# A decoder kernel with one engine's program written out in the Mamba stage, and one transposition moved in the feed-forward stage

## The reference, cut to what matters

```python
# Mamba layer, cut: 512 inner channels, 16 states
dt = softplus(log_dt @ W_dt.T + b_dt)
A_bar, Bu = exp(dt[..., None] * A), dt[..., None] * B_coef[:, :, None, :] * xc[..., None]
h = A_bar_t * h + Bu_t                      # for each position t
y_t = sum over states of h * C_t
y = (y + xc * D) * silu(z)
# quantised feed-forward, cut: 256 -> 1024 -> 256
def bitlinear(x, w): return act_quant(x) @ weight_quant(w).T
out = bitlinear(silu(bitlinear(x, w_gate)) * bitlinear(x, w_up), w_down)
```

## Time and profile before

| what | value |
|---|---|
| median of 3 runs | 3803.97 us (3803.84 to 3806.27) |
| the profiled execution, its own time | 3800.63 us |
| span of its trace, first to last instruction | 3797.8 us |
| mean granted TensorE clock | 0.95 of full speed |
| PE, DVE, ACT, POOL busy, share of the span | 87%, 82%, 74%, 68% |

### The profile page before, as it was taken

The page is one execution under the profiler, slowest core; times in us unless marked ns, Lnnn a source line. Parts: engine busy times, 40 slices in busy tenths (PEclk is TensorE's granted clock), DMA queues, the critical chain, the costliest instruction groups (busy, mean ns, idle before and its releaser), DMA issues. The chain is left out here.

```text
span 3797.8 us, 75246 instructions
## 1 busy us (share of the span) xinstructions
PE 3290.3 (87%) x23328; PEld 2494.5 (66%) x23360; DVE 3118.3 (82%) x5163; ACT 2817.2 (74%) x5141; POOL 2567.5 (68%) x2971
## 2 busy tenths in 40 slices
PE   8996988979963688999988989898899879997887
PEld 5664666668542477777767777777777757775565
DVE  5665999955386699999899989989999849998887
ACT  2222777854475799899898998989899737776887
POOL 1222767730086599888888988898898936665676
PEclk9998999979976899999999999999999989998999
DMA  2112222242213111121111211111111112322111
GB/s 61 55 55 56 44 53 49 50 106 46 52 34 85 37 52 57 50 54 53 54 53 56 57 50 57 49 53 56 55 52 51 48 47 68 77 54 64 51 61 45
DMA packets 285549, 209.62 MB, mean 55 GB/s; under 512 B 131416, under 2 KB 249752, under 8 KB 285224
## 3 DMA queue, kind: packets, MB, share of 16 engines
q1 hardware_dynamic: 285224, 205.72, 19.9%
HBM read 149.18 MB, written 51.41 MB: 53 GB/s over the span
## 5 line engine op out<-in xcount | busy, mean ns | idle before, releaser
L2896 POOL TENSOR_TENSOR ma_ch<-ma_h,ma_crep 128x512 f32<-128x512 f32 x1024 | 1348.2, 1340 | 190.5 <-DVE ma_h L3007 159.8
L3007 DVE TENSOR_TENSOR_SCAN ma_h<-ma_a,ma_pbu 128x512 f32<-128x512 f32 x1024 | 1196.5, 1203 | 123.5 <-PE ma_pbu L2576 108.1
L2576 PE MATMUL ma_pbu<-ma_ident,ma_bu 128*128 128x128 f32 x4096 | 655.6, 284 | 120.6 <-DVE ma_h L3007 92.6
L2576 PEld LDWEIGHTS ma_pbu<-ma_ident,ma_bu 128*128 128x128 f32 x4096 | 481.5, 144 | 349.2 <-DVE ma_h L3007 204.3
L2785 ACT ACTIVATE ma_a<-ma_dt,ma_A 128x510 f32<-128x510 f32 x1024 | 672.8, 711 | 1.3 <-issue 1.3
L2585 PE MATMUL ma_py<-ma_ident,ma_ch 128*128 128x128 f32 x4096 | 623.9, 278 | 9.8 <-DVE ma_gT L3025 7.8
L2778 ACT ACTIVATE ma_bu<-ma_uT,ma_b_t 128x512 f32<-128x512 f32 x864 | 555.6, 711 | 13.0 <-PE ma_pbu L2576 11.3
L2585 PEld LDWEIGHTS ma_py<-ma_ident,ma_ch 128*128 128x128 f32 x4096 | 493.4, 145 | 14.3 <-DVE ma_gT L3025 11.4
L1576 POOL TENSOR_TENSOR xa_prob<-xa_e,xa_rec_head 128x616 f32<-128x616 f32 x128 | 155.6, 1217 | 126.4 <-DVE xa_rec_head L1668 114.2
L924 POOL TENSOR_TENSOR xa_prob<-xa_e,xa_rec_head 128x616 f32<-128x616 f32 x128 | 155.7, 1217 | 107.0 <-DVE xa_rec_head L1016 90.4
L362 POOL TENSOR_TENSOR la_veps<-la_mv,la_eps 128x2 f32<-128x2 f32 x32 | 6.3, 196 | 248.8 <-DVE la_mv L395 248.8
(11 more groups left out here) (375 smaller groups left out, 7942.3 us busy)
## 6 DMA issues: line engine op xcount, KB each, us to landing
ma_crep<-ma_ct_dram SPq DMA_DIRECT2D x256, 256.0 KB
xa_x<-act SPq DMA_DIRECT2D x64, 256.0 KB, 2.7
act<-xa_y SPq DMA_DIRECT2D x64, 256.0 KB, 2.2
la_x<-in_x SPq DMA_DIRECT2D x32, 256.0 KB, 2.8
act<-la_y SPq DMA_DIRECT2D x32, 256.0 KB
act<-ea_x SPq DMA_DIRECT2D x32, 256.0 KB, 4.0
ma_x<-act SPq DMA_DIRECT2D x16, 512.0 KB, 4.5
ma_xr<-act SPq DMA_DIRECT2D x16, 512.0 KB
```

What stands on the lines that cost most here:

```text
L2576: last = pe.transpose(pbu[c % 2][:, t * P:(t + 1) * P], bu[:, s % 2, t, c * P:(c + 1) * P], ident[:, :])
L2896: pool.tensor_tensor(ch[:, s % 2, c], h[:, s % 2, c], crep[:, s % 4, :], ALU.mult).then_inc(multiplied, 1)
L3007: dve.tensor_tensor_scan(out=h[:, s % 2, c, :], data0=a[:, s % 2, c, :], data1=pbu[c % 2][:, :], initial=0.0, op0=ALU.mult, op1=ALU.add).t ...
```

## The change

Two edits, both in PE's programs. In the Mamba stage PE's 16 groups are written out one behind the other, with constant parity and constant wait values; the other engines keep their loops. In the feed-forward `turn_x` of an even slot moves from behind the up projection to behind the gate projection.

```diff
@@ mamba, TensorE
-            groups(pe, group)
+            for g in range(NG):
+                group(g, g % 2, g == 0, g == NG - 1)
             for late in range(K - LAG, K):
@@ bit_ffn, TensorE, slot
                     pe.wait_ge(g_ready, count(n2))
                     project(n2, 0, pgate, gate_made)
+                if not odd and n4 is not None:
+                    turn_x(n4)
                 if n is not None:
                     turn_h(n)
                 if n_1 is not None:
@@
                     pe.wait_ge(h_ready, count(n2))
                     project(n2, 1, pup, up_made)
-                if not odd and n4 is not None:
-                    turn_x(n4)
```

## The result

The changed kernel takes 3776.13 us, the median of 4 runs (3772.69 to 3779.92), against 3803.9 us (3802.32 to 3806.27, 4 runs) for the kernel before: a ratio of 0.9927, interval 0.991 to 0.9944. The forecast was 3786 us in a range of 3774 to 3797. In two later comparisons the changed kernel took 3776.78 and 3776.36 us, so its time is firm; the kernel before took 3798.2 and 3799.9 there (3797.4 and 3800.4 in two more), so the gain is 27.8 us in the first comparison and 21.4 and 23.5 us in the other two. The kernel before was at its slowest in the first.

What follows compares the result with a forecast made beforehand. Bounds: feed-forward, a PE-ACT wait cycle with DVE next; Mamba boundaries, PE's and DVE's jumps. Gains 13.5 + 4.4 = 17.9 us: span 3797.8 - 17.9 = 3779.9, + 2.8 = 3782.7, + 3.3 to the median: 3786 us, range 3774 to 3797.

Steps and rivals of the forecast that it cites:

- two bounds: Feed-forward: the PE-ACT wait cycle at 8.09 us a pair and DVE's work at 8.12, expected to coincide; 8.17 taken.
- DVE's own 8.12: Feed-forward: DVE idles 0.50 us of each 8.62 us pair, so a pair cannot go below 8.12 us.
- the ring: Feed-forward: the cycle of waits through PE and ACT from even ph to even ph, forecast at 4.12 + 3.97 = 8.09 us.
- 0.05 us a pair: Feed-forward: allowance for two closing bounds disturbing one another, in the 8.17 us taken for a pair.
- B: Feed-forward: another wait, say DVE's hscale, closes the cycle; gain only 0.1 us a pair, time 3797 us; chance 0.10.
- C: Feed-forward: px ahead of even ph costs 0.34 us a pair, not returned; time 3810 or 3814 us; chance 0.05.
- the sixth jump's price: Mamba: at the sixth jump only PE still jumps, so writing it out returns the whole 2.4 us.
- So I take 0.4 us at each of the five: Mamba: where DVE's jump stays, removing PE's returns 0.4 us each, between 0 and 1.2; 2.0 us in all.
- up to 8 us: Mamba: the gain if PE keeps its full clock after standing for DVE.
- The mid-group row: Mamba: profile row where PE, after standing 2.83 us far from any jump, ran at 1.2 GHz for 3.3 us.
- Rival A: Mamba: PE's jumps were the whole stall, so all 14.6 us return; time 3776 us; chance 0.20.
- Rival D: Mamba: the written-out program starves PE of instructions, 0.5 us in each of 16 groups; time 3794 us; chance 0.02.

Runs made afterwards that it cites:

- px_twice: The changed kernel with the four px transpositions done twice at their new place; 3785.43 us (one run).
- dve_no_jump: The changed kernel with DVE written out in both the Mamba stage and the feed-forward; 3768.64 us, ratio 0.992.
- mamba_only: The kernel before with only PE's 16 Mamba groups written out, feed-forward unchanged; 3792.46 us, ratio 0.9984.
- dve_alone: The kernel before with DVE's Mamba groups written out instead of PE's, feed-forward unchanged; 3804.94 us, ratio 1.0018.

## Why the prediction was right, and where it was off

**Feed-forward, 13.5 us forecast, 14.1 measured.** Right in size, and by its own steps. ACT's wait for `px` is gone, `xT` follows `scaled`, and PE's way from odd to even `ph` took on the `px`. The pair was forecast at 8.17 us from two bounds, a ring of 8.09 and DVE's own 8.12. Measured are 8.00 for the ring (`px_twice`: 8.44 less the 0.44 added) and 8.14 for DVE in the loop. `dve_no_jump` shows DVE's share of the bound: written out, DVE needs no more than 8.00 either. So the two bounds do stand on top of each other there, as forecast, each about 0.1 us lower. What was not foreseen is that part of DVE's 8.12 is not its work but its loop. That the two bounds disturb one another, for which 0.05 us a pair had been added, did not show: from the third to the 61st `h` a pair took 8.13 us on average, 8.60 before. PE's stand of 0.40 us ahead of the odd `ph` belongs to the ring as forecast (4.12 us for 3.53 of work, measured 4.09). Rivals B and C are refuted: ACT did wait for `hscale`, but 6.8 us in all, where B and C needed the whole gain to go there.

**Mamba, 4.4 us forecast, 7.1 measured in the profiled pair, 5.8 in the medians of `mamba_only`.** The mechanism was right: DVE's jump stays and is as long as before, the sixth jump's price came back but for 0.5 us (112.87 to 110.92 us, 2.0, forecast 2.4), and PE stands for DVE. The mis-sized step is this term: "So I take 0.4 us at each of the five". It took the half clock behind DVE's stand as certain, from a row of a stand in mid-group. The runs showed it in 11 of 30. Worked out: in the loop a jump cost 2.59 us on average (12 of them), 15.5 us for six. Written out, 5 x (0.37 x 2.5 + 0.63 x 1.1) + 0.3 = 8.4 us. The gain is then 7.1 us, and the six written-out traces have it: 1741.4 on average against 1748.7 for the two with the loop, 7.3 us. By these prices most of the gain at the five jumps is not time in which DVE waited for PE's branch, but a slow stretch of PE that often did not come. Had the half clock been certain, it would have been 15.5 - 5 x 2.5 - 0.3 = 2.7 us. The prediction had named this way out, "up to 8 us", and given it no chance of its own. One reading in it is off without effect: PE's median branch of 3574 ns counts the seventh, which falls through; the six that jump have 3768.

The mid-group row was a poor model for the jumps. In the six written-out traces PE stands 2.7 us in mid-group 78 times, and 72 of these stands have the half clock within the 5 us behind them. Here is one of them in the changed kernel, and the stand behind the fifth jump, with a window of 5 us behind each:

```profile
2460.35 0.63 PE L2576 MATMUL ma_pbu<-ma_ident,ma_bu 128*128 128x128 f32 x4 [2.68 <-DVE ma_h L3008]
...
2499.37 0.66 PE L2576 MATMUL ma_pbu<-ma_ident,ma_bu 128*128 128x128 f32 x4 [2.70 <-DVE ma_h L3008]
```

```profile
2460.30:2465.30 5.00, 4.81 (x28) 4.44 (x29) 5.00 (x9) 5.00 (x8) 4.85 (x5) 0.66 0.09 33
...
2499.40:2504.40 5.00, 5.00 (x44) 4.76 (x45) 4.72 (x5) 3.15 (x6) 4.85 (x4) 1.00 0.14 54
```

The stands are equally long and the outcome differs.

**Rival A is refuted, although its number, 3776, is the measured time.** It said that PE's jumps were the whole stall and 14.6 us would return. `mamba_only` gave 5.8 us, DVE still stands at five jumps, and `dve_alone` shows the reverse case: PE's jump alone costs all that the two cost together. **Rival D** is refuted too: a stretch without a jump takes 110.16 us with PE written out and took 110.32 before.

**From 3782.7 to the median.** The two stages gave 21.2 us for 17.9 forecast. The span was forecast at 3779.9 and came at 3778.1; the profiled execution was forecast at 3782.7 and took 3779.92 (1.8 us outside the span in place of 2.8). The other 7.1 us of the miss are in the step from there to the median: before, the profiled execution stood 3.3 us below it, after, 3.8 us above. The draw of the clock at five jumps, 1.4 us each, explains a spread of that size, up to 7 us between none and all; that it is what happened in these very runs is not shown, since only one of them has a trace.

**Luck in the range.** The range for the forecast by itself was 3781 to 3796 us, and the median of 3776.13 lies below it. It lies within 3774 to 3797 only because the range was stretched to take in rival A's lower end, and rival A is refuted. By stages the steps held, each gain inside its own bounds; that the total did too is partly luck.

**Not settled.** Why DVE's written-out groups take 0.4 us longer in the Mamba stage, while its written-out waits save 0.14 us a pair in the feed-forward. And what decides whether the clock is halved after a stand. Neither the length of the stand nor the kernel alone does; where it stands matters (72 of 78 in mid-group, 11 of 30 behind DVE's jump, 16 of 18 behind PE's own jump, with `dve_alone`), and no run shows why. That the 1.4 us between the two prices are caused by the clock is read from the windows and prices together; no run sets the clock.

## What to carry to other kernels

Where several engines jump back at the same point of a loop, their jumps run beside each other, and writing one engine out returns little more than the difference between the longest and the next (here the rest was a slow stretch of PE that often did not come); read each engine's branch and the first instruction behind it before pricing. Of the ways to be rid of the rest, more groups a turn kept the fast body and the short jumps elsewhere; writing every engine out in the Mamba stage alone gave the gain back and more (3779.97 us against 3776.78); writing DVE out in both stages was the fastest (3768.64). When an in-order engine waits for a transfer between two others, moving its producer is worth the ring's saving less what the producer costs in its new place, down to the next engine's own time; doubling the moved work shows at once whether it is on the ring.

## What the hardware showed that was not expected

- The same small loop's jump on DVE took 0.3 us or 3.3 to 3.6 us, with nothing changed but what was written ahead of it.
- A taken jump over the Mamba body, from branch to the first instruction of the new turn, took 3.4 to 4.2 us on DVE, 3.4 to 4.4 on PE, 2.5 to 3.5 on POOL, 2.4 to 2.9 on ACT, and 0.2 to 0.3 on SP.
- After a stand of 2.5 to 3.3 us behind DVE's jump PE had half the clock in 11 of 30 cases, in traces of one kernel 3 of 5 and 1 of 5; after one of 2.7 us in mid-group, in 72 of 78. The Trainium skill, "TensorE: Matmul & The Clock Gate", part 1, says that how many matmuls run slow at a kernel's start differs from run to run of the same kernel. The traces show such a difference in mid-kernel too, and here it goes with 1.4 us each time, on average.
- Writing out a program is not always faster for the engine that runs it: 0.4 to 0.55 us a group the wrong way on DVE, with the same work.
